# A decoder kernel on one core: new PSUM banks and a new order in the multi-query attention, and one load block for x and the first weights

## The reference

```python
x = x + _L0_attn_ref(_layernorm(x), w_qkv, w_o, qn_g, qn_b, kn_g, kn_b)   # 16 query heads, 4 key heads of 128 (GQA)
x = x + _L0_xattn_ref(_layernorm(x), ctx, ctx)
x = x + _L0_ffn_ref(_layernorm(x), ...)
x = x + _L1_attn_ref(_layernorm(x), Wqkv_w, Wqkv_b, out_w, out_b)         # 16 query heads of 16, one key head (MQA)
x = x + _L1_xattn_ref(_layernorm(x), ctx, ...)
x = x + _L1_ffn_ref(_layernorm(x), ...)

# _L1_attn_ref
qkv = einsum('bsd,ed->bse', x, Wqkv_w) + Wqkv_b      # 256 query, 16 key, 16 value columns
scores = einsum('bqhd,bkd->bhqk', q, k) * scale      # causal mask
attn = softmax(scores)
ctx = einsum('bhqk,bkd->bqhd', attn, v)
out = einsum('bsd,ed->bse', ctx, out_w) + out_b
```

## Time and profile before

| | us |
|---|---|
| median of 3 runs (lowest, highest) | 3246.2 (3240.28, 3254.96) |
| the profiled execution | 3244.57 |
| its span, first to last instruction | 3242.8 |
| PE / DVE / ACT / POOL busy, share of the span | 82% / 63% / 49% / 42% |
| mean granted TensorE clock | 0.937 of full |

### The profile page before, as it was taken

One profiled execution on the slowest core, in us unless ns is written; L12 is line 12 of the kernel. 1 busy time (PEld: TensorE's weight loads), 2 busy tenths in 40 slices (PEclk: granted clock), 3 DMA queues, 4 the chain that ended last, 5 costly groups with the idle time before them and its releaser, 6 DMA issues. The chain is left out here.

```text
span 3242.8 us, 85996 instructions
## 1 busy us (share of the span) xinstructions
PE 2653.5 (82%) x33006; PEld 1936.8 (60%) x33006; DVE 2034.8 (63%) x3734; ACT 1574.7 (49%) x2946; POOL 1358.5 (42%) x1483
## 2 busy tenths in 40 slices
PE   1888888888858888867677779999999999996565
PEld 1667777777732222224466667888888888885333
DVE  4888888888857888848577743434334343434676
ACT  2555555555527777731233314344443434442565
POOL 1888888888832333314222212222222222220665
PEclk9899999999978999979799989999999999998576
DMA  3000000000013333300000020000000000000000
GB/s 119 2 1 0 0 0 0 0 0 0 0 36 91 92 92 92 90 13 0 27 26 26 26 68 6 7 5 7 6 7 7 6 7 5 7 4 28 13 16 23
DMA packets 94784, 77.50 MB, mean 24 GB/s; under 512 B 17520, under 2 KB 88560, under 8 KB 93424
## 3 DMA queue, kind: packets, MB, share of 16 engines
q1 hardware_dynamic: 94576, 74.35, 7.5%
HBM read 55.97 MB, written 17.04 MB: 23 GB/s over the span
## 5 line engine op out<-in xcount | busy, mean ns | idle before, releaser
L1319 DVE TENSOR_REDUCE x_mx<-x_ps 128x2 f16<-128x512 f32 x512 | 330.9, 682 | 49.7 <-PE x_ps L1383 47.5
L1288 ACT ACTIVATE x_e<-x_ps 128x512 f32<-128x512 f32 x512 | 292.0, 596 | 49.7 <-PE x_ps L1387 33.8
L365 POOL TENSOR_TENSOR x1s<-x1s,x1mx 128x1024 f32<-128x1024 f32 x32 | 60.8, 1901 | 541.9 <-DVE x1mx L361 541.9
L1383 PE MATMUL x_ps<-x_k,x_q 32*128 32x256 f16 x1024 | 196.1, 285 | 81.2 <-ACT x_e L1288 50.7
L1642 ACT ACTIVATE x_q<-x_ps,x_q_bias,x_q_scale 128x128 f32<-128x128 f32 x512 | 185.7, 467 | 158.3 <-PE x_ps L105 158.3
L435 ACT CAST x1oh<-x_ps 128x1024 f16<-128x1024 f32 x64 | 64.7, 1012 | 329.9 <-PE x_ps L427 329.9
L103 PE MATMUL a_ps<-ln_xha,a_wq 128*128 128x128 f16 x1024 | 180.2, 222 | 51.2 <-ACT a0v L605 44.1
L1383 PEld LDWEIGHTS x_ps<-x_k,x_q 32*128 32x128 f16 x1024 | 58.3, 93 | 263.4 <-DVE x_mx L1319 130.6
L554 POOL TENSOR_TENSOR a_w<-a_qsw,a_tab 128x512 f32<-128x512 f32 x128 | 176.7, 1380 | 57.4 <-ACT a_qsw L615 56.1
L1387 PE MATMUL x_ps<-x_q,x_k 32*128 32x256 f16 x1024 | 197.8, 287 | 1.7 <-ACT x_e L1288 1.4
L105 PE MATMUL x_ps<-x_chi,x_w 128*128 128x128 f16 x1024 | 181.3, 221 | 17.2 <-issue 17.2
(11 more groups left out here) (360 smaller groups left out, 9110.7 us busy)
## 6 DMA issues: line engine op xcount, KB each, us to landing
x_q<-x_q_rows SPq DMA_DIRECT2D x32, 256.0 KB, 2.8
x_k<-x_k_rows SPq DMA_DIRECT2D x32, 256.0 KB, 3.1
a_stage<-in_x_w SPq DMA_DIRECT2D x32, 256.0 KB, 2.6
x_vt<-in_ctx_v SPq DMA_DIRECT2D x32, 144.0 KB, 2.3
x_wt<-in_x_wt SPq DMA_DIRECT2D x4, 1028.0 KB, 5.7
x_all<-in_x SPq DMA_DIRECT2D x8, 512.0 KB, 8.0
x_cf<-in_ctx SPq DMA_DIRECT2D x32, 128.0 KB, 2.1
x_q_rows<-x_xhl SPq DMA_DIRECT2D x32, 128.0 KB, 1.7
```

The lines of the kernel that those rows point to most:

```text
L1288: act.activation(e[:, u % ES].rearrange("p c n -> p (c n)"), s2_ps(u), ACT.Exp, scale=XT ** -0.5).then_inc(e_ready, 1)
L1319: dve.reduce_max(mx[:, p % 2, c:c + 2], s1_ps(u), AX).then_inc(mx_ready, 1)
L1383: return pe.matmul(s1_ps(u)[:, c], q[r, p % 4, g, c * P:(c + 1) * P], k[r, p % 4, g], start=True, stop=True)
```

## The change

**Multi-query attention.** The transposed exponentials (`ptp`) get banks 2 and 3 for themselves, the scores keep 4 and 5; the attention output's transpose (`ot_ps`) moves behind the products in bank 7, and `y` behind the layer norm's transpose in bank 0. `scores` of a tile now waits for the subtraction of the tile before (`s_ready`) and no longer for the copy of its transposed exponentials. Each engine's list is reordered: PE starts a step with the scores; the products stay one tile behind; output and its high and low halves are two tiles behind; the layer norm's transpose is done two tiles ahead.

```diff
-        ot_ps = ps[:, 2, 0:2 * P].rearrange("p (b n) -> p b n", b=2)
-        y = ps[:, 3, 0:DM]
+        ot_ps = ps[:, 7, P:3 * P].rearrange("p (b n) -> p b n", b=2)
+        y = ps[:, 0, DM:2 * DM]
         sc = ps[:, 4:6, :].rearrange("p a (h s) -> p (a h) s", s=SEQ)
-        ptp = ps[:, 4:6, :].rearrange("p a (h s) -> p (a h) s", s=P)
+        ptp = ps[:, 2:4, :].rearrange("p a (h s) -> p (a h) s", s=P)
...
             def step(t, p, has_next):
                 if started(t, 1):
                     copy_transposed(t - 1)
+                if started(t, 2):
+                    high(t - 2)
                 if has_next:
                     ln.high(act, t + 1, 1 - p, proj_ready)
                     query_key(t + 1, 1 - p)
                 exponential(t)
-                if started(t, 1):
-                    high(t - 1)
...
             def step(t, p, has_next):
                 ch.tile(t)
+                if started(t, 2):
+                    low(t - 2)
                 if has_next:
                     ln.low(dve, t + 1, 1 - p)
+                if further(t):
+                    ln.stats(dve, ch, t + 2, p)
+                maximum(t)
                 if started(t, 2):
                     add(t - 2)
-                if further(t):
-                    ln.stats(dve, ch, t + 2, p)
+                if has_next:
+                    values(t + 1, 1 - p)
+                if started(t, 1):
+                    weights_low(t - 1, 1 - p)
                 if further(t):
                     ln.normalise(dve, t + 2, p)
-                maximum(t)
                 if started(t, 1):
                     divide(t - 1)
-                if has_next:
-                    values(t + 1, 1 - p)
                 denominator(t)
-                if started(t, 1):
-                    low(t - 1)
-                if started(t, 1):
-                    weights_low(t - 1, 1 - p)
...
             def scores(t, p):
                 pe.wait_ge(kd_ready, t + 1)
                 if started(t, 1):
-                    pe.wait_ge(pt_ready, t)
+                    pe.wait_ge(s_ready, t)
...
             def transpose(t):
                 pe.wait_ge(e_ready, t + 1)
-                pe.wait_ge(s_ready, t + 1)
+                wait_used(pe, pt_ready, t, 1)
...
                 wait_used(pe, o_ready, t, 1)
+                wait_used(pe, ol_ready, t, 1)
...
             def step(t, p, has_next):
-                if started(t, 1):
-                    transpose(t - 1)
-                if has_next:
-                    ln.transpose(pe, t + 1, 1 - p)
+                scores(t, p)
+                if has_next:
+                    pe.wait_ge(ln.xl_ready, t + 2)
                 if started(t, 2):
                     output(t - 2)
                 if has_next:
                     front(t + 1, 1 - p)
-                scores(t, p)
                 if started(t, 1):
                     products(t - 1, 1 - p)
+                transpose(t)
+                if further(t):
+                    wait_used(pe, x_done, t, 2)
+                    ln.transpose(pe, t + 2, p)
+                if started(t, 1):
                     transpose_o(t - 1)
```

```diff
         @block.sync
         def _(sp):
             sp.dma_start(m.ident[:, :], m.d["ident"]).then_inc(id_in, 16)
-            for s in range(0, TILES, 4 if TILES >= 4 else TILES):
-                n = min(4, TILES)
-                sp.dma_start(m.x_all[:, s:s + n, :],
-                             m.d["x"][s * P:(s + n) * P, :].rearrange("(t p) d -> p t d", p=P)).then_inc(x_in, 16)
-            sp.wait_ge(x_in, 16 * (TILES // min(4, TILES)))
+            sp.wait_ge(id_in, 16)
...
+def load_gqa(m, d, wq, wk, wv, wo, rope, gb, mask, x_first, x_in, const_in):
...
+            sp.dma_start(st["q0"][:, :], half(d["a0_q"], 0)).then_inc(loaded["q0"], 16)
+            sp.dma_start(st["q1"][:, :], half(d["a0_q"], 1)).then_inc(loaded["q1"], 16)
+            sp.dma_start(st["k"][:, :], d["a0_k"]).then_inc(loaded["k"], 16)
+            load_x(0, x_first)
+            sp.dma_start(st["v"][:, :], d["a0_v"]).then_inc(loaded["v"], 16)
+            sp.dma_start(st["o0"][:, :], half(d["a0_o"], 0)).then_inc(loaded["o0"], 16)
+            sp.dma_start(rope[:, :, :], d["rope"]).then_inc(const_in, 16)
+            sp.dma_start(gb[:, :], d["a0_gb"]).then_inc(const_in, 16)
+            sp.dma_start(mask[:, :], d["causal"]).then_inc(const_in, 16)
+            sp.dma_start(st["o1"][:, :], half(d["a0_o"], 1)).then_inc(loaded["o1"], 16)
+            for i in range(1, TILES // X_PIECE):
+                load_x(i, x_in)
+            sp.wait_ge(const_in, 48)
...
+        @block.scalar
+        def _(act):
+            for i, (n, (hi, lo)) in enumerate(order):
+                if n in centre:
+                    act.wait_ge(centred, i + 1)
+                    act.copy(hi, st[n][:, :]).then_inc(high_done, 1)
+                else:
+                    act.wait_ge(loaded[n], 16)
+                    act.activation(hi, st[n][:, :], ACT.Copy, scale=WS).then_inc(high_done, 1)
...
+                dve.reduce_sum(mean[:, 0:heads], w, AX).then_inc(summed, 1)
+                dve.wait_ge(summed, i + 1)
+                dve.tensor_scalar(mean[:, 0:heads], mean[:, 0:heads], WS / P, None, ALU.mult).then_inc(mean_set, 1)
+                dve.wait_ge(mean_set, i + 1)
+                dve.scalar_tensor_tensor(w, w, WS, spread(mean[:, 0:heads], P), ALU.mult, ALU.subtract).then_inc(centred, 1)
+                dve.wait_ge(centred, i + 1)
+
+            for i, n in enumerate(centre):
+                centre_heads(i, n)
+            for i, (n, (hi, lo)) in enumerate(order):
+                if n not in centre:
+                    dve.wait_ge(high_done, i + 1)
+                    dve.scalar_tensor_tensor(lo, st[n][:, :], WS, hi, ALU.mult, ALU.subtract).then_inc(wide_low_done, 1)
+
+        @block.gpsimd
+        def _(pool):
+            for i, (n, (hi, lo)) in enumerate(order):
+                if n in centre:
+                    pool.wait_ge(high_done, i + 1)
+                    pool.tensor_tensor(lo, st[n][:, :], hi, ALU.subtract).then_inc(low_done, 1)
```

More of the change, by code:

```diff
@@ L535, in _ @@
         def _(sp):
[L536 to L539 removed]
+            sp.wait_ge(x_in, 16 * (TILES // X_PIECE - 1))
         @block.gpsimd
@@ L700, in head @@
                 tables()
+                dve.wait_ge(x_first, 16)
                 ln.stats(dve, ch, 0, 0)
@@ L729, in step @@
                 if further(t):
+                    if isinstance(t, int) and t == 1:
+                        dve.wait_ge(x_in, 16 * (TILES // X_PIECE - 1))
                     ln.stats(dve, ch, t + 2, p)
@@ L2117, in _ @@
             copy_transposed(TILES - 1)
+            high(TILES - 2)
             high(TILES - 1)
```

55 lines of the change are left out of this document (39 added, 16 removed).

## The result

The changed kernel takes 3228.1 us (median of 20 runs, 3214.33 to 3251.89), the kernel before 3248.78 (20 runs, 3240.28 to 3261.96). The ratio is 0.9939, with a 95% interval of 0.9921 to 0.9957: faster by 0.6%, some 20 us, where 90 were forecast. The profiled execution took 3251.45 with a span of 3249.4 and is one of the slowest of the 20, so first it must be seen where its time lies.

| from start to first statistics, then stages, us | before | after | difference |
|---|---|---|---|
| start | 57.67 | 39.72 | -18.0 |
| grouped-query attention | 884.5 | 886.2 | +1.7 |
| first cross attention | 484.5 | 511.6 | +27.1 |
| low-rank layer | 120.8 | 120.7 | -0.1 |
| multi-query attention | 361.9 | 355.3 | -6.6 |

A forecast was written before the change was run, and what follows sets the result against it. The prediction took a closed chain of waits, no engine full, to set the attention's 10.25 us tile, and loading to hold the start. 3244.57 less 66.7 (attention) and 23.0 (start) gave 3154.9, median 3156 us, range 3138 to 3179.

The forecast's parts named there:

- The order and its chain: Multi-query attention: a new chain from scores through products, `values`, `weights_low`, `normalise`, `divide` and `transpose_o` sets the tile, 8.08 us.
- the old chain: Attention loop before: a closed chain of waits through transpose, copy, layer norm, `front`, scores and softmax, given as 10.23 us.
- 8.1 and 66.7: Multi-query attention: 8.1 us a tile in place of 10.25, over 31 steps 66.7 us saved.
- Every instruction keeps its shape and bank width, so I keep its duration: Multi-query attention: old durations carried into the new order, among them `weights_low` 0.68 and `ln.normalise` 0.41 us.
- tail behind the products: Attention tile: hand-overs, `values`, `weights_low`, `normalise`, `divide` and `transpose_o` from the products' end to the next scores, 1.94 us.
- The clock rival: Attention loop: TensorE falls to its lower clock, 13.9 us a tile, 3336 us in all; chance 0.03.
- rows 1: Profile of the old attention loop: no engine full, PE busy 213 of 270 us, at the full clock.
- Fill and drain: Attention stage's half-clock first tiles and its drain: same pieces in either order, so the same cost.
- The start: Load block before the first statistics: these come at 34.7 us in place of 57.67, 23.0 us saved.
- with POOL free of charge DVE ends the block at 30.0: Load block's lower bound: DVE's own work ends at 30.0 us, against 31.3 for POOL's end.
- The transfers hid: Start: weights landed by 25.5 us and the last of x by 39, both hidden behind other work.
- The sum: Whole kernel: 3244.57 - 66.7 - 23.0 = 3154.9 us for the profiled execution, median 3156 us.

The follow-up runs named there:

- e11: Changed kernel with DVE's attention step reordered, q/k low halves on DVE instead of POOL, and two added matmuls in PE's gap: 3183.11 us, ratio 0.9799.
- e13: e11 with ten more matmuls once, ahead of the first tile of the multi-query attention: 3140.58 us, ratio 0.9678.
- e5: Changed kernel with four added matmuls per attention step on PE, in the gap behind the transpose of the exponentials: 3175.41 us, ratio 0.9762.
- e4: Changed kernel with `weights_low` moved to the end of DVE's attention step: 3199.64 us, ratio 0.9842.
- e6: Changed kernel with `normalise` between maximum and subtraction, `add` cut in two, its second part and `weights_low` last in DVE's step: 3175.48 us, ratio 0.9784.
- e8: Kernel before with one DVE memset on its own buffer added to each attention step: 3263.8 us.
- e3: Kernel before with the new start (load block) alone, attention as before: 3228.91 us, ratio 0.9922.
- e1: The changed kernel again, unaltered, for a second trace: 3234.84 us.

## Why the prediction was wrong, step by step

- **The order and its chain: right.** The new wait is `values` on the products, 0.59 to 0.81 us in every step. Scores wait for nothing but PE's own list. From the start of the scores to that of the products it takes 4.18 us (1708.09 to 1712.27), exactly the 2.28 + 0.66 + 1.24 of the sum, at the full clock. The chain also passes through `normalise`, `divide` and `transpose_o` as forecast, though PE's wait shows ahead of the layer norm's transpose. (The pieces given for the old chain add to 10.28, not 10.23; the old tile has 10.21 and 10.28 in turn, so the reading stands.)
- **That e11 and e13 run a tile of 8.12 and e13's stage is 67.5 us shorter, where 8.1 and 66.7 were forecast, is luck.** They have another order: PE waits for nothing in their loops, so PE's own list sets the tile, 7.7 us and 0.43 for the two added matmuls. The forecast's chain was never run without its two faults; with the hand-overs as measured it would be about 8.3, by my estimate from 8.08 and the 0.2 of the next point.
- **"Every instruction keeps its shape and bank width, so I keep its duration": this step failed.** Of the tail behind the products (forecast 1.94, from their end to the scores) the trace has 2.72 (1705.37 to 1708.09): `weights_low` took 1.25 up to its successor in place of 0.68, the rest are hand-overs, 0.2 together. In the tile after, it took 1.45. The shortest tiles of the loop are 9.07 in place of 8.1 (e5, at the full clock throughout, has 9.06 and 9.3); 31 x 0.97 = 30 us. From e5 to e11, both at the full clock, the stage falls by 30.6 us, from 322.3 to 291.7. The duration was true where the row stood (1711.63), with POOL idle; I moved the operation beside POOL's keys and took its price along. e4 and e6 show it. The row to ask for was what ran on POOL at the time, and the same operation in another stage: the normalisation, whose 0.41 the sum also used, takes 1.15 beside POOL in the trace of before.
- **The clock rival: put at 0.03, and it came half true.** The argument against it was "the old loop held the full clock with 2.2 us of waits in 10.25, and the new one has 0.5 in 8.1". Less waiting, yet the clock fell, so the amount of waiting does not decide. Nor does a wait of 1 us behind thin work as such: the old loop had one too, 1.03 behind the products in every tile, at the full clock. What differs is the order around it (now products, transposes and then the wait), and which part of that matters stays open. Its price was not the 3.6 us a tile of that rival, since the clock returns every time: 10.15 to 10.18 less 9.07 to 9.17 is 1.0 to 1.1 us a tile, 31 to 34 us. e5 measured 33.0. e8 shows that rows 1 could not carry the argument: 1.00 in a row doesn't say how near the edge it is.
- **Fill and drain**: taken as equal, and the parts ahead of the first maximum and behind the last are (21.5 and 18.8 us before, 21.1 and 19.3 now). The half-clock tiles at the start were not: the first two tiles take 18.4 us in place of 24.8. That is 6.4 of the 6.6 us gained; the other 29 tiles gave 0.2.
- **The start: 18.0 in place of 23.0.** The same cause. POOL was sized too high (5.5 at 2048 columns; 4.06 and 4.63 measured) and its end was right by chance, 31.6 against 31.3. The step that failed is the lower bound "with POOL free of charge DVE ends the block at 30.0": beside POOL it ended at 35.95, and the block change took 3.77 in place of 3.37. The first transfer went out at 3.38, sooner than the 4.2 taken. The 4497 ns quoted from the Trainium skill, "GPSIMD Engine Reference", section "Performance versus the Vector engine", were near the measured 4.06 and 4.63. What they gave for the end, 28.7, was not, as the third piece started late, at 28.50.
- **The transfers hid**, as forecast: the grouped-query attention is 886.2 against 884.5, about as e3 (883.8).
- **The sum** forecast -89.7 for the profiled execution, which came out 6.6 longer by its span. I had no term for the first cross attention, whose clock was 0.60 in the stretch shown above and 1.00 in the kernel before. The two traces of the changed kernel (the second is e1) differ by 16.7 us, and this stage by 16.9. Of the other executions only the mean clock is known: 0.931 in the shortest, 0.907 in the longest. How much of it the median carries is not shown.

A rule that spoke against this change stood in the Trainium skill, and I had not weighed it: "GPSIMD Engine Reference", section "Specifications", says that GpSimd's interfaces to SBUF are shared with VectorE and that it contends with instructions in a 2-port mode or with two SBUF inputs; "SBUF — State Buffer", section "SBUF: two separate sides", says that whoever starts first holds the pair for the whole instruction. The trace agrees: 3.74 us for 16 columns, until POOL is done; 1.33 to 1.53 for `weights_low`; and 1.22 to 1.23, undisturbed, for the maximum and the subtraction that read PSUM. That the 16-column operation and the normalisation, which read one tile each, run in such a mode is not shown by any row; their durations fit it.

## What to carry to other kernels

A duration belongs to a place: before an operation of DVE is moved, look at what runs on POOL at its new place, and find the operation, or one of its kind, beside POOL somewhere in the trace that is already there. Operations that read PSUM were not held in this kernel, nor was the sum over the exponentials (L379), which reads one tile in SBUF: 1.22 with POOL at work and without. A row that says 1.00 for TensorE's clock tells nothing of how near the edge it is. Compare tiles one by one, since several lengths in one loop give the clock away; where it swings, try a few matmuls that PE has time for in the wait behind the thin work. And after any change read the stages that weren't touched: a wait on "issue" in a loop, with packets of the instruction queue beside it, is the place of the code, and a change ahead of it can give or take 1%.

## What was unexpected of the hardware

- Some operations of DVE are held until POOL's ends: 3.74 us for 16 columns (0.17 without POOL), 1.53 for 0.68, 1.21 for 0.41.
- TensorE's clock fell in a loop in which PE was busy 89% of the time (71.12 of 80), and held with four matmuls more in the gap. The old order kept it with PE busy 79% (213.31 of 270) at 10.25 us a step, and lost it at 10.51. In e6 it fell with no wait of PE over 0.34.
- The same code in one stage took from 1038 to 1088 us, by the number of instructions ahead of it.
- **Still open**: why the clock of the first cross attention, whose code is the same in all kernels, is 1.00 in some stretches and 0.60 in others, which makes 480 to 512 us of it; and what exactly in the succession of thin work and waiting makes the clock fall. Neither was tried by itself.
